# A recommendation tower on one core: feature interaction rewritten by chunk, with gathers at most three chunks ahead

## The reference

```
x = layer_norm(dense_t @ Wd.T, gd, bd)                                # dense vector, E = 128
y = layer_norm(jnp.einsum('bnd,ed->bne', sparse_t, Ws), gs, bs)       # 26 gathered rows
y = layer_norm(jnp.einsum('bne,pn->bep', y, Wsi), gsi, bsi)           # mixed to 32
T = jnp.concatenate([x[:, None, :], swapaxes(y, 1, 2)], axis=1)       # 33 vectors
Zflat = jnp.einsum('bnd,bmd->bnm', T, T)[:, TRIL_I, TRIL_J]           # 528 products
z = layer_norm(Zflat @ Wl.T, gl, bl)[:, :384]
h = jnp.maximum(jnp.concatenate([z, r_dense_t], axis=1) @ W_top1 + b_top1, 0.0)
h = jnp.maximum(h @ W_top2 + b_top2, 0.0)
y = h @ W_top3
```

## Time and profile before

| | |
|---|---|
| median of 3 runs | 244.02 us (243.06 to 245.71) |
| the profiled execution | 243.04 us |
| its span, first to last instruction | 241.2 us |
| mean granted TensorE clock | 0.83 |
| PE busy | 173.7 us, 72% |
| PEld busy | 131.6 us, 55% |
| DVE busy | 121.1 us, 50% |
| POOL busy | 108.1 us, 45% |
| ACT busy | 76.2 us, 32% |
| DMA | 8.14 MB, mean 34 GB/s |

### The profile page before, as it was taken

How to read it: one execution, slowest core, us unless ns; L and a number is a source line. 1 busy time by engine, 2 the same in 40 slices (tenths; PEclk the granted TensorE clock), 3 DMA queues, 4 the chain that set the end, 5 groups by cost and what they waited for, 6 DMA issues and landing times.

```text
span 241.2 us, 4708 instructions
## 1 busy us (share of the span) xinstructions
PE 173.7 (72%) x1983; PEld 131.6 (55%) x1983; DVE 121.1 (50%) x225; ACT 76.2 (32%) x158; POOL 108.1 (45%) x110
## 2 busy tenths in 40 slices
PE   0668825649981954689558728979929799867896
PEld 0318721235551724458528518846729686767695
DVE  6474400238958270546482920916863984773012
ACT  2021400026684420515321310414414165350224
POOL 3787777727775173456570660557450000330000
PEclk9985555757996796899875955997967999999999
DMA  6515453101111010010110010011010000000000
GB/s 190 178 24 125 111 155 97 45 5 26 28 22 29 3 30 16 14 22 16 20 26 8 16 24 6 11 24 22 16 27 0 0 0 1 0 3 5 0 3 0
DMA packets 5728, 8.14 MB, mean 34 GB/s; under 512 B 2357, under 2 KB 3279, under 8 KB 5712
## 3 DMA queue, kind: packets, MB, share of 16 engines
q0 software_dynamic: 3328, 3.41, 7.4%
q1 hardware_dynamic: 1664, 3.65, 5.0%
q10 hardware_dynamic: 720, 0.85, 1.2%
HBM read 7.91 MB, written 0.00 MB: 33 GB/s over the span
## 4 chain that ended last, share of the span: by engine, by line
PE 53%; issue 17%; another core or an unknown queue 13%; DVE 9%; ACT 5%; DMA 2%; ACTq 1%; DVEq 0%
PE ps_z L990 8%; PE ps_gq L947 6%; PE ps_y L968 5%; PE ps_ut L958 5%; PE ps_tail L1045 4%; PE ps_tail L1022 3%; PE ps_z L1002 3%; PE ps_tail L899 2%; DVE var L701 2%; DMA gs_sb<-in_gs_row_dram 2%; PE ps_y L1022 2%; PE ps_gq L941 2%; PE ps_tail L931 2%; PE ps_tail L1054 1%
## 5 line engine op out<-in xcount | busy, mean ns | idle before, releaser
L285 POOL DMA_INDIRECT G<-in_table_dram,idx x104 | 104.0, 1000 | 74.9 <-PE ps_ut L958 41.7
L990 PE MATMUL ps_z<-V 128*32 128x34 f32 x1024 | 21.1, 218 | 28.0 <-issue 26.3
L673 DVE TENSOR_TENSOR qg<-ps_gq,G 128x384 f32<-128x384 f32 (+1 forms) x16 | 9.4, 588 | 57.0 <-PE ps_gq L947 23.2
L990 PEld LDWEIGHTS ps_z<-V 128*32 128x32 f32 x1024 | 16.9, 128 | 35.3 <-issue 32.3
L968 PE MATMUL ps_y<-ut,wcg 64*128 64x512 f32 x64 | 21.6, 751 | 7.2 <-issue 7.0
L958 PE MATMUL ps_ut<-S,G 128*128 128x192 f32 (+4 forms) x128 | 25.1, 348 | 2.2 <-DVE G L686 1.5
L947 PE MATMUL ps_gq<-gram,gt 128*128 128x128 f32 x104 | 19.2, 335 | 8.9 <-ACT gt L367 7.7
L958 PEld LDWEIGHTS ps_ut<-S,G 128*128 128x128 f32 x128 | 23.5, 229 | 3.2 <-DVE G L686 2.1
L701 DVE TENSOR_REDUCE var<-sq 128x32 f32<-128x1024 f32 x16 | 19.4, 1213 | 8.5 <-ACT sq L381 7.9
L381 ACT ACTIVATE sq<-V 128x1024 f32<-128x1024 f32 x16 | 16.9, 1058 | 20.3 <-DVE V L696 20.3
L947 PEld LDWEIGHTS ps_gq<-gram,gt 128*128 128x128 f32 x104 | 16.4, 236 | 10.5 <-ACT gt L367 7.8
(11 more groups left out here) (138 smaller groups left out, 228.3 us busy)
## 6 DMA issues: line engine op xcount, KB each, us to landing
G<-in_table_dram,idx POOLq DMA_INDIRECT x104
w1z<-in_w_z_dram SPq DMA_DIRECT2D x1, 768.0 KB
wl<-in_wl_blocks_dram SPq DMA_DIRECT2D x1, 768.0 KB
dns<-in_dense_t_dram ACTq DMA_DIRECT2D x1, 512.0 KB
w1d<-in_w_d_dram SPq DMA_DIRECT2D x1, 512.0 KB
wl<-in_wl_blocks_dram SPq DMA_DIRECT2D x1, 512.0 KB
w2s<-in_w_dram SPq DMA_DIRECT2D x1, 512.0 KB
wrow<-in_wsi_rows_dram SPq DMA_DIRECT2D x1, 208.0 KB
```

The lines of the kernel that those rows point to most:

```text
L285: pool.indirect_dma_start(G[:, j, g, :], None, table, bass.IndirectOffsetOnAxis(ap=idx[:, k:k + 1], axis=0)).then_inc(gathered[c], 16)
L990: mm = pe.matmul(ps_z[32 * qb:32 * qb + 32, bb // 8, col:col + SLOTS], V[:, b, 0:NPROJ], V[:, b, :], start=True, stop=True)
```

## The change

- `G` gets room for all four groups. The gathers of chunk n wait until `embed` of chunk n-3 is done (`AHEAD = 3`), where they waited for `project_fields` of chunk n-4.
- `V` holds two samples side by side: ones, two dense vectors, 2 x 32 vectors. One matmul of 64 x 67 makes the products of two samples (and products across the two, which are not used); two such matmuls stand side by side in the array. `pair_products` runs for every chunk, 16 matmuls each.
- `z_evacuate` and `z_merge` run for every chunk, in two and four instructions.
- For groups 0 to 2 SP moves the kept products into `zb` and `zx` with 24 DMAs a group (`move_pairs`), in place of `spread_pairs` and ACT's copies. The last group keeps the matmuls.
- For groups 0 to 2 `project_pairs` has the samples on the partitions: 5 matmuls of 512 columns. The squares are summed by ACT as it makes them, ACT scales the features, PE transposes them in three matmuls, and ACT copies them.
- The loop is written out; the steps of slot n are in `slot(n)`. `prepare_b1` moves behind the second chunk's `gram_rows`. All of `prepare_dense` uses the bank `ps_tail`. POOL does the second scaling for one chunk of the last group.

```diff
 CHUNK = 2 * CB
-POOL_CHUNKS = (1, 2)
+NCHUNK = NG * NC
+AHEAD = 3
 SPAN = 6
-SLOTS = NPROJ + 2
-X_SLOT, ONE_SLOT = NPROJ, NPROJ + 1
+SLOTS = 3 + 2 * NPROJ
...
+            def move_pairs(gp):
+
+                sp.wait_ge(z_merged, (gp + 1) * NC)
+                for qb in range(4):
+                    src = zt[32 * qb:32 * qb + 32, gp % 2, :, qb % 2, :]
+                    at = slice(gp * GRAN + 32 * qb, gp * GRAN + 32 * qb + 32)
+                    for q in range(4):
+                        sp.dma_start(zb[32 * q:32 * q + 32, :, at], src[:, PQ * q:PQ * q + PQ, :]).then_inc(z_moved, 16)
+                    sp.dma_start(zx[ROW_XV:ROW_XV + 32, at], src[:, RING, :]).then_inc(z_moved, 16)
+                    sp.dma_start(zx[ROW_S:ROW_S + 32, at], src[:, RING + 1, :]).then_inc(z_moved, 16)
+
+            for gp in range(NG - 1):
+                move_pairs(gp)
 
...
             pool.wait_ge(idx_ready, 1)
-
-            for gp in range(NG):
-                for c in range(NC):
-                    if gp:
-
-                        pool.wait_ge(ut_ps, nth(gp - 1, c))
-                    for j in batch(c):
-                        for g in range(2):
-
-                            k = gp * 2 * TILES + 2 * j + g
-                            pool.indirect_dma_start(
-                                G[:, j, g, :], None, table,
-                                bass.IndirectOffsetOnAxis(ap=idx[:, k:k + 1], axis=0)).then_inc(gathered[c], 16)
-
-            for n, c in enumerate(POOL_CHUNKS):
-                pool.wait_ge(r2_ready, nth(NG - 1, c))
-                pool.tensor_tensor(chunk_v(c), chunk_v(c), r2_pool[:, n, :].unsqueeze(2).broadcast_to([P, CHUNK, NPROJ]),
-                                   ALU.mult).then_inc(v_pool_ready, 1)
+            for n in range(NCHUNK):
+                if n >= AHEAD:
+
+                    pool.wait_ge(y_ps, 2 * (n - AHEAD) + 2)
+                for j in batch(n % NC):
+                    for g in range(2):
+
+                        k = n // NC * 2 * TILES + 2 * j + g
+                        pool.indirect_dma_start(
+                            G[:, n // NC, j, g, :], None, table,
+                            bass.IndirectOffsetOnAxis(ap=idx[:, k:k + 1], axis=0)).then_inc(gathered[n // NC][n % NC], 16)
+
...
+            def z_evacuate(n):
+
+                if n >= 2 * NC:
+                    act.wait_ge(z_moved, (n // NC - 1) * MOVES * 16)
+                act.wait_ge(z_ps, n + 1)
+                for w in range(2):
+                    last = act.copy(z_places(n, w), z_pairs(w)[:, :, :, 0:RING])
+                last.then_inc(z_first, 1)
+
+            def f_squares(gp):
                 act.wait_ge(f_ps, gp + 1)
-                act.activation(f_sq[:, :, :], bank, ACT.Square).then_inc(f_sq_ready, 1)
...
+                act.activation(f_sq[:, :, :], tail, ACT.Square, accum_out=f_sum[:, :]).then_inc(f_sq_ready, 1)
+
+            def deviation3(gp):
+                act.wait_ge(f_sq_ready, gp + 1)
+                act.activation(sd3[:, 0:1], f_sum[:, :], ACT.Sqrt, bias=eps[:, :], scale=1.0 / L).then_inc(sd3_ready, 1)
+
...
+            def z_merge(n):
+
+                dve.wait_ge(z_first, n + 1)
+                for w in range(2):
+                    dve.copy_predicated(z_places(n, w), mmask[:, :].unsqueeze(1).unsqueeze(1).broadcast_to([P, 4, 2, RING]),
+                                        z_pairs(w)[:, :, :, RING:NPROJ])
+                x_at, s_at = (zt[:, n // NC % 2, m, :, n % NC * 8:n % NC * 8 + 8].rearrange("p l (w s) -> p w s l", w=2)
+                              for m in (RING, RING + 1))
+                dve.tensor_copy(x_at, z_slots[:, :, :, 1:3])
+                dve.tensor_copy(s_at, z_slots[:, :, :, 0:1].broadcast_to([P, 2, 4, 2])).then_inc(z_merged, 1)
+
...
+            def pair_products(n):
+                if n == NCHUNK - 2:
+
+                    pe.wait_ge(v_pool_ready, 1)
                 else:
-                    pe.wait_ge(v_ready, nth(gp, 2 * h + 1))
...
+                    pe.wait_ge(x_sd_ready, 1)
                 else:
 
-                    pe.wait_ge(z_merged, nth_half(gp, h) - 1)
-                    if h == 0:
-                        pe.wait_ge(z_sb, gp)
-                for bb in range(16):
-                    for qb in range(4):
-                        b = h * HALF + 16 * qb + bb
-                        col = (bb % 8) * SLOTS
-                        mm = pe.matmul(ps_z[32 * qb:32 * qb + 32, bb // 8, col:col + SLOTS], V[:, b, 0:NPROJ],
-                                       V[:, b, :], start=True, stop=True)
+                    pe.wait_ge(z_merged, n)
+                for w in range(2):
+                    for s in range(4):
...
+            def project_pairs(gp):
+
+                pe.wait_ge(wl_ready, 2)
+                pe.wait_ge(dense_ready, OC1)
+                if gp > 0:
+                    pe.wait_ge(yo_ready, gp)
+
+                pe.wait_ge(z_moved, (gp + 1) * MOVES * 16)
+                at = slice(gp * GRAN, (gp + 1) * GRAN)
+                for k in range(KB):
+                    mm = pe.matmul(ps_tail[:, :], zb[:, k, at] if k < PB else zx[:, at], wl[:, k, :],
+                                   start=(k == 0), stop=(k == KB - 1))
+                mm.then_inc(f_ps, 1)
...
+            def slot(n):
+                gp, c = divmod(n, NC)
+                transpose_rows(n)
+                project_fields(n - 1)
+                gram_rows(n)
+                if n == 3:
+                    prepare_dense(1)
+                if n == 4:
                     prepare_last_block()
...
+                if n == 5:
+                    prepare_dense(2)
+                if n == 6:
+                    prepare_dense(3)
+                if c == 3 and gp > 0:
+                    project_pairs(gp - 1)
+                if c == 0 and gp > 1:
+                    transpose_features(gp - 2)
+                if c == 1 and gp > 1:
+                    layer2(gp - 2)
+                embed(n - 1)
+                pair_products(n - 2)
+                if c == 0 and gp > 1:
+                    layer1(gp - 2)
+                if c == 1 and gp > 1:
+                    layer3(gp - 2)
 
...
```

More of the change, by code:

```diff
@@ L60 @@
 KB = PB + 1
+MOVES = 24
 LC, LLIVE = L // P, LIVE // P
@@ L901, in prepare_b1, with prepare_xsum @@
                 mm.then_inc(b1_ps, 1)
+            def prepare_xsum():
+                pe.wait_ge(b1_ready, 1)
+                pe.matmul(ps_tail[ROW_X:ROW_X + 1, :], ones[:, 0:1], x_sb[:, :], start=True, stop=True).then_inc(xsum_ps, 1)
             def prepare_dense(oc):
@@ L942, in transpose_rows, with gram_rows @@
                 mm.then_inc(gt_ps, 1)
-            def gram_rows(gp, c):
-                pe.wait_ge(gt_sb, nth(gp, c))
-                for n in range(len(batch(c))):
-                    mm = pe.matmul(ps_gq[:, n * P:(n + 1) * P], gt[:, n * P:(n + 1) * P], gram[:, :], start=True, stop=True)
+            def gram_rows(n):
+                pe.wait_ge(gt_sb, n + 1)
+                for i in range(rows_of(n)[2]):
+                    mm = pe.matmul(ps_gq[:, i * P:(i + 1) * P], gt[:, i * P:(i + 1) * P], gram[:, :], start=True, stop=True)
@@ L1040, in layer1, with transpose_features @@
+            def transpose_features(gp):
+                pe.wait_ge(f_ready, gp + 1)
+                for k in range(LLIVE):
+                    mm = pe.transpose(tail[:, k, :], f_scaled[:, k, :], eye[:, :])
+                mm.then_inc(ft_ps, 1)
             def layer1(gp):
```

774 lines of the change are left out of this document (320 added, 454 removed).

## The result

The changed kernel took **271.18 us** (median of 4 runs, 268.30 to 272.04) against 244.87 for the kernel before in the same comparison: a ratio of 1.106 (95% interval 1.094 to 1.118), 10.6% slower. The forecast was 255. The direction was right, and the loss is 2.4 times the one forecast. The profiled execution took 272.04 us, with a span of 270.2 us.

A forecast was written before the change was run, and what follows sets the result against it. Bound: gather bursts on POOL, each letting PE run about 100 instructions before stopping it. Stretches 38.5 + 159 (97.5 + 16.5 + 45) + 55 = 252.5 us, 254.3 with 1.84 around the span, said as 255; range 212 to 272.

The forecast's parts named there:

- The start: Stretch from kernel start to the end of the first embed: 38.5 us where it was 51.5, a gain of 13.
- The cost of the release: Gathers wait for a later embed, so PE's steps before it run while POOL idles; called the costing part, not priced alone.
- The step that failed: VectorE's work: merging 0.9 us a chunk instead of 0.3, offset by removed feature work; even at 29 us a group.
- The light cycles: Chunks without projection or layers: 100 PE instructions are spent before the embed, leaving 1.5 us outside the burst.
- The heavy cycles: Chunks with extra PE work: 6 us outside the burst with the wide projection, 6 to 7 with the layers.
- the 14.4: Excess in us of the middle stretch, first embed to thirteenth: forecast 159, measured 173.4.
- an allowance of 100 records: During a burst of gathers PE gets about 100 instructions, then nearly none until 1.2 to 1.5 us after its end.
- Rival C: Kept products moved by DMA come late: each wide projection waits 9 us, two of three pay, 273 us; chance 0.08.
- Rival A: Same pace as today: PE's saved instructions offset the later release, 1.84 us a gather, 241 us; chance 0.27.
- Rival B: PE's stops during bursts go, so light cycles run at POOL's pace of 1.25 us a gather, 210 us; chance 0.19.
- The end: Stretch from the thirteenth embed to the end: 55 us against 53.3 before, 1 to 2 added by three more merges.

The follow-up runs named there:

- the reordered kernel: The changed kernel with the same operations in another order on VectorE, ScalarE and TensorE, projection and layers behind the embed: 221.88 us, and 223.17 in another group, both without stops.

## Why the prediction was right or wrong

**The start** came out near (forecast 38.5, measured 37.0), in part by luck. The shorter first burst is right (it ends at 30.62, forecast 30.64), and so are the steps up to the gram matmuls (29.1, forecast 29.9). Behind them two misses cancel. The bias product took 2.74 us where the sum had 5.1 and 1.4 of stop, and then PE stood for 3.2 us, for which the sum has nothing. The first embed also waits for the dense vector (`x_ready`), and VectorE finishes that only behind the second chunk's variance (whose input it gets at 31.28, behind the burst) and the scaling of its rows:

```profile
34.22 0.55 DVE L633 TENSOR_SCALAR x_sb<-x_sb,sm 128x512 f32<-128x512 f32 x1
34.86 2.08 PE L915 MATMUL ps_y<-ut,wcg 64*128 64x512 f32 x4 [3.18 <-issue]
```

**The cost of the release** was called "the part that costs". In the kernel before it costs 12.2 us on a chip with stops. In the changed kernel undoing it gives nothing that can be told (3.5 us, across two groups). On a chip without stops it costs the kernel before nothing, and the reordered kernel neither. That the forecast's 11 us for everything are close to the 12.2 is a coincidence.

**The step that failed** is one sentence under *DVE*: "DVE comes out even, at some 29 us a group, and is not the bound". It compared busy times. The busy time moved by 16.6 us (121.1 to 137.7), and the merge was mis-sized by half a microsecond (0.9 us forecast; 187.87 to 189.21, 1.34, measured). What the sum left out is the order. The diff writes each engine's slot out, and going round VectorE's slot with ScalarE's three answers (squares and two roots) gives 8.9 us a chunk, from durations that but for the new merge were in the trace of before. Gram, projection, layer 2 and embed stand in the same round, so their time and their waits are added to it. That VectorE is on it, the run without the masked copies shows: 14.1 us less. The same operations in an order with those answers covered take 8.0 to 8.3 us a light chunk, and the kernel 30 us less. From the first embed to the thirteenth the changed kernel takes 13.1 us a chunk on a chip without stops, the reordered one 10.1 to 10.4 and the kernel before 8.3. What lies between the last two was not isolated; the reordered kernel's projections still wait 13.6 us for the moves in one profile of it.

**The light cycles** were forecast at 10.5 us (6 gathers 7.5, plus 1.5, plus 1.5) and measured at 10.0 to 11.7. That the number fits is a coincidence: without gathers the later ones take 6.6 to 7.1 us from embed to embed (less than the chain's 8.9, since an embed can run ahead of its bias add, and the debt is paid in the next, heavy cycle), and with them the chain of VectorE and the late results of TensorE fill the time, not the gathers.

**The heavy cycles** carry the rest of the miss. With the projection I forecast 17.5 us (10 + 1.5 + 6) and 22.5 and 20.9 came; with layer 2, 15.5 and 17.6 and 18.0 came. That is 8.4 and 4.6 us, 13 of the 14.4. In the two with the projection its 10 records took 6.0 and 7.0 us for 4.56, and waits for the moves of 3.1 and 0.6 were not in the sum; what was in it, an allowance of 100 records used up, was not what held the gram matmul, as PE had 60 and 72 records in these bursts.

**Rival C** (the moves late) had 0.08 and was to decide from 0.61 us a DMA on. An issue every 0.65 us is just beyond that, and by the rival's own sum (24 × 0.65 + 2.3 = 17.9 against 17) worth 0.9 us a projection, not its 9. But the slack was mis-sized as well: a light slot is 8.9 us without stops, and the moves were waited for in every projection, 16.2 us in all there and 4.5 with stops. So the mechanism is real and its price was wrong. **Rival A**'s mechanism (fewer instructions on PE help) did not show; no run isolates it. **Rival B** (the stops go) was put down to instruction counts. Stops do go, but by the group and its chip, and then the kernel before gains some 56 us and the changed one 12 to 19, so the change looks worse, not better.

**The end** was 4.8 us longer than forecast: the last chunks run the same chain, and 59.0 us in the changed kernel without stops (53.0 in the kernel before) say that the stops have no part in it.

## What to carry to other kernels

An engine that is half busy can still be the bound. Where a change rewrites the order of the slots, walk once round the slot over all engines with the durations of before, adding each answer that another engine must give, and compare that with the busy time; here it was 8.9 us against 7.0. Then add whatever stands in the same line in a heavy slot, and what it waits for; here that made 14 to 22 us. Put what the next round waits for (the copy that feeds the gram matmul) ahead of what only this round needs, and a long product behind the embed that others wait for. And 24 small DMAs from one queue are a latency of 24 issues, to be compared with the slot and not with their share of bandwidth.

## What the runs showed of the hardware that was not expected

- The same kernel took 243 to 245 us in three groups of runs and 187.7 to 187.9 in two, each on another chip and each run within 1.1% of its group's median. The gathers' own durations are nearly the same on both (1000 and 1027 ns on average, 1.25 us apart). On the first kind TensorE's results can reach other engines as late as the end of a burst of gathers (7.3 us late for the transposes at 164.03), on the second PE runs through the two bursts shown at full clock. What differs between the groups was not found.
- On a chip with stops, pauses of 0.54 us behind every second gather let 208 records of PE and PEld through in 7.6 us and made the kernel before 4.7% faster; one pause per burst did not. That it is the density of gathers which counts is argued from these two runs only.
- The count of about 100 records, on which the prediction was built, was seen in the kernel before and not in the changed one (58 to 91 records at the longest gap in ten of the thirteen bursts from the fourth on; but where there are no stops its longest gap in several bursts comes after 60 to 72 records too, while PE waits for ScalarE's copy, so these counts are not those of a limit). With the late results in view, it is more likely the work that PE can start before its first results are handed over than an allowance. No run tested that.
- No version beats the kernel before on both kinds of chip: the one with pauses wins 4.7% with stops, and was not run without them, where GpSimd is the bound. By an estimate the 36 pauses would cost about 18 us there: with stops a gather behind a pause starts 1.76 us after the one before, without a pause 1.25.
